# Splitting the rows of maxima on VectorE ahead of the turn, in the first attention stage as in the second

## The reference, cut to what matters

```
x = L0_attn_x                                    # (4, 1024, 128) float32
xn = layernorm(x)
s = L0_attn(xn, ...)                             # 16 heads of 8, bias by relative position
g = silu(L0_ffn(xn, ...))
x = x + s * g
xn = layernorm(x)
s = L1_attn(xn, ...)                             # 8 differential heads, causal
g = silu(L1_ffn(xn, ...))                        # 8 experts, top 2
return x + s * g

def L0_attn(x, Wq, bq, Wk, bk, Wv, bv, Wo, bo, rel_table):
    Q, K, V = proj(Wq, bq), proj(Wk, bk), proj(Wv, bv)
    rel_emb = rel_table[clip(pos[:, None] - pos[None, :] + 127, 0, 254)]
    scores = (einsum('bhid,bhjd->bhij', Q, K) + einsum('bhid,ijd->bhij', Q, rel_emb)) / sqrt(8)
    attn = softmax(scores, axis=-1)
    out = einsum('bhij,bhjd->bhid', attn, V)
    return out @ Wo.T + bo
```

## Time and profile before

| | us |
|---|---|
| median of 3 runs | 2022.06 |
| the 3 runs | 2018.59 to 2034.35 |
| the profiled execution, its own time | 2009.26 |
| its span, first to last instruction | 2007.4 |

### The profile page before, as it was taken

How to read it: one execution, slowest core, us unless ns; L and a number is a source line. 1 busy time by engine, 2 the same in 40 slices (tenths; PEclk the granted TensorE clock), 3 DMA queues, 4 the chain that set the end, 5 groups by cost and what they waited for, 6 DMA issues and landing times. The chain is left out here.

```text
span 2007.4 us, 77167 instructions
## 1 busy us (share of the span) xinstructions
PE 1620.5 (81%) x33422; PEld 1255.6 (63%) x33422; DVE 1322.0 (66%) x1921; ACT 1171.6 (58%) x1500; POOL 1098.2 (55%) x1104
## 2 busy tenths in 40 slices
PE   6888789989999999999997633487778778778776
PEld 4666677777787777788785523376445545555554
DVE  5553767778777767768786342255877677677673
ACT  2333477777787777778785321154556556556555
POOL 4755488888899788978986265001222222222211
PEclk9888799999999999999998665698799799788788
DMA  3355023222332233322221172362121121111100
GB/s 96 97 172 141 24 90 92 75 82 77 103 99 55 82 94 97 86 65 66 74 70 56 57 215 82 100 176 75 40 51 29 44 50 28 49 47 27 30 13 10
DMA packets 189005, 151.47 MB, mean 75 GB/s; under 512 B 92163, under 2 KB 178190, under 8 KB 183166
## 3 DMA queue, kind: packets, MB, share of 16 engines
q1 hardware_dynamic: 161526, 103.80, 18.2%
q10 hardware_dynamic: 20088, 27.00, 4.3%
q0 software_dynamic: 7056, 15.74, 2.7%
HBM read 98.91 MB, written 46.79 MB: 73 GB/s over the span
## 5 line engine op out<-in xcount | busy, mean ns | idle before, releaser
L1876 ACT ACTIVATE a_EX<-bank 128x1024 f32<-128x1024 f32 x624 | 615.0, 1027 | 296.9 <-PE bank L1672 233.0
L2015 DVE TENSOR_TENSOR a_PM<-bank,a_PM 128x1024 f32<-128x1024 f32 x336 | 400.6, 1222 | 121.7 <-PE bank L1672 110.1
L1797 POOL TENSOR_TENSOR a_SN<-a_SN,a_MB 128x1024 f32<-128x1024 f32 x176 | 420.8, 2431 | 41.8 <-DMA a_MB<-m_dram 40.6
L2039 DVE TENSOR_REDUCE a_M<-bank 128x2 f32<-128x1024 f32 (+3 forms) x296 | 330.9, 1163 | 111.2 <-PE bank L1685 74.3
L1975 PE MATMUL bank<-a_EX,VV 128*32 128x128 f32 x9984 | 378.8, 294 | 11.1 <-issue 9.2
L1672 PE MATMUL bank<-QS,KS 51*128 51x128 bf16 (+1 forms) x4992 | 248.4, 233 | 95.0 <-DVE a_M L2039 33.0
L1975 PEld LDWEIGHTS bank<-a_EX,VV 128*32 128x32 f32 x9984 | 279.3, 117 | 62.7 <-issue 36.1
L1672 PEld LDWEIGHTS bank<-QS,KS 51*128 51x128 bf16 (+1 forms) x4992 | 163.9, 101 | 191.0 <-DVE a_M L2039 54.0
L1872 ACT ACTIVATE a_SN<-bank 128x1024 f32<-128x1024 f32 x176 | 176.8, 1024 | 61.0 <-PE bank L1651 59.3
L1651 PE MATMUL bank<-QP,rel_t 112*128 112x32 bf16 x5632 | 198.1, 177 | 3.7 <-issue 3.4
L1880 ACT ACTIVATE a_SN<-a_SN 128x1024 f32<-128x1024 f32 x176 | 184.3, 1058 | 22.8 <-POOL a_SN L1797 22.7
(11 more groups left out here) (213 smaller groups left out, 2286.5 us busy)
## 6 DMA issues: line engine op xcount, KB each, us to landing
a_MB<-m_dram SPq DMA_DIRECT2D x32, 1024.0 KB, 5.3
QS<-q_dram SPq DMA_DIRECT2D x192, 96.0 KB, 3.0
q_dram<-t_PARTS SPq DMA_DIRECT2D x32, 192.0 KB, 3.0
k_dram<-t_PARTS SPq DMA_DIRECT2D x16, 384.0 KB, 3.7
KS<-k_dram ACTq DMA_DIRECT2D x16, 384.0 KB
xs_dram<-bv SPq DMA_DIRECT2D x26, 192.0 KB, 4.8
t_XS<-xs_dram SPq DMA_DIRECT2D x18, 256.0 KB, 4.1
y_dram<-t_Y ACTq DMA_DIRECT2D x18, 256.0 KB, 2.3
```

What stands on the lines that cost most here:

```text
L1797: pool.tensor_tensor(near_view(sn), near_view(sn), as_near(MB[:, :, :], it.part), ALU.add)\
L1876: act.activation(as_banks(EX[:, it.need % ER[layer]], part), by_head, ACT.Exp, scale=SCALE).then_inc(act_done, 1)
L2015: dve.tensor_tensor(pm, mb.rearrange("p hh (k i) -> p hh k i", k=4), pm, ALU.max).then_inc(max_used, 1)
L2039: dve.tensor_reduce(target[:, :, p0:p0 + g], mb[:, :, 0:g * width].rearrange("p hh (k j) -> p hh k j", k=g), AX.X, ALU.max).then_inc(max_u ...
```

## The change

In the first attention stage `maxt` reduces into `MT`, the tile with room for three parts, and behind the second half DVE does what it does in the second stage: cast to bfloat16, subtract, cast the rest, subtract, each with a drain (`split_rows`). PE turns 48 columns instead of 16. ACT copies the turned rows twice: to `MP` in bfloat16 and to `MR` in float32. The step `msplit` on POOL goes. SP sends two DMAs instead of six. `mstore` becomes two DMAs of 8 rows each instead of one of 16. The planner's costs follow: `mstore` 400 to 800, `mcopy` 277 to 540 in this stage, `rows` 4000 to 1600, 1100 more on DVE for the second half of `maxt`, and no POOL step between `mcopy` and the rows. The due times in `AIM` stay.

```diff
-COST = {..., "mstore": 400, ...
-        ..., "mcopy": 277,
+COST = {..., "mstore": 800, ...
+        ..., "mcopy": (540, 277),
...
-        ..., "rows": (4000, 1600), ...
+        ..., "rows": 1600, ...
...
-                taken.append(ring(Step("maxt", u, None, c), COST["maxt"], "dve", COST["take"],
+                taken.append(ring(Step("maxt", u, None, c), COST["maxt"], "dve", COST["take"] + 1100 * c,
...
-        done["msplit", u] = add("pool", Step("msplit", u), COST["split"], [(copied, told)]) if layer == 0 else copied
-        rows = [(add("sp", Step("msplit", u), COST["rows"][layer], [(done["msplit", u], told)]), COST["rows_in"])]
+        done["msplit", u] = copied
+        rows = [(add("sp", Step("msplit", u), COST["rows"], [(done["msplit", u], told)]), COST["rows_in"])]
...
                         if it.kind == "msplit":
-                            sp.wait_ge(m_split if layer == 0 else m_copied, u + 1)
+                            sp.wait_ge(m_copied, u + 1)
                             for hh in range(2):
                                 row = hh * HALF + ROWS
-                                if layer == 0:
-                                    for k in range(3):
-                                        sp.dma_start(QS[row + k:row + k + 1, u % QR, :, hh, :], MP[hh * PAIRS:(hh + 1) * PAIRS, u % 2, k, :])\
-                                          .then_inc(m_in[u % QR], 16)
-                                else:
-                                    sp.dma_start(QS[row:row + 3, u % QR, :, hh, :], MP[hh * 3 * PAIRS:(hh + 1) * 3 * PAIRS, u % 2, :])\
-                                      .then_inc(m_in[u % QR], 16)
+                                sp.dma_start(QS[row:row + 3, u % QR, :, hh, :], MP[hh * 3 * PAIRS:(hh + 1) * 3 * PAIRS, u % 2, :])\
+                                  .then_inc(m_in[u % QR], 16)
...
-                            sp.dma_start(m_dram[u % 2].rearrange("(k hh i) -> hh k i", hh=2, i=P), MR[:, u % 2, :]).then_inc(m_stored, 16)
+                            for hh in range(2):
+                                sp.dma_start(m_dram[u % 2].rearrange("(k hh i) -> hh k i", hh=2, i=P)[hh],
+                                             MR[hh * 3 * PAIRS:hh * 3 * PAIRS + PAIRS, u % 2, :]).then_inc(m_stored, 16)
...
-                        elif it.kind == "msplit":
-                            mp = MP[:, u % 2, :, :]
-                            pool.wait_ge(m_copied, u + 1)
-                            pool.tensor_copy(mp[:, 0], MR[:, u % 2, :])
-                            pool.drain()
-                            pool.tensor_tensor(MS[:, :], MR[:, u % 2, :], mp[:, 0], ALU.subtract)
-                            pool.drain()
-                            pool.tensor_copy(mp[:, 1], MS[:, :])
-                            pool.drain()
-                            pool.tensor_tensor(mp[:, 2], MS[:, :], mp[:, 1], ALU.subtract).then_inc(m_split, 1)
...
-                                    act.wait_ge(m_split, u - 1)
-                                    act.wait_ge(m_stored, 16 * (u - 1))
-                                act.activation(MR[:, u % 2, :], bank[0:H, MISC, 0:P], ACT.Copy, scale=-1.0).then_inc(misc_used, 1)
+                                    act.wait_ge(m_stored, 32 * (u - 1))
+                                act.activation(MP[:, u % 2, :], bank[0:3 * H, MISC, 0:P], ACT.Copy, scale=-1.0)
+                                act.activation(MR[:, u % 2, :], bank[0:3 * H, MISC, 0:P], ACT.Copy, scale=-1.0).then_inc(misc_used, 1)
...
+                    def split_rows(u):
+
+                        top, rest, last = (MT[:, u % 2, :, k, :] for k in range(3))
+                        dve.tensor_copy(MH[:, :, :], top)
+                        dve.drain()
+                        dve.tensor_tensor(rest, top, MH[:, :, :], ALU.subtract)
+                        dve.drain()
+                        dve.tensor_copy(MH[:, :, :], rest)
+                        dve.drain()
+                        dve.tensor_tensor(last, rest, MH[:, :, :], ALU.subtract)
+                        dve.drain()
+                        dve.sem_inc(m_ready, 1)
...
-                            dve.tensor_reduce(M[:, u % 2, :].rearrange("p (hh k) -> p k hh", hh=2)[:, 4 * part:4 * part + 4, :],
+                            dve.tensor_reduce(MT[:, u % 2, :, 0, :].rearrange("p hh k -> p k hh")[:, 4 * part:4 * part + 4, :],
                                               mb.rearrange("p b (k hh j) -> p (b k) hh j", k=2, hh=2), AX.X, ALU.max).then_inc(max_used, 1)
                             if it.last:
                                 dve.drain()
-                                dve.sem_inc(m_ready, 1)
+                                split_rows(u)
```

More of the change, by code:

```diff
@@ L133, in far_keys @@
     return [(0, width)] if width <= 512 else [(0, 512), (512, width)]
-COST = {"far": 270, "near": 1290, "maxt": 880, "mstore": 400, "mb": 700, "av": 930, "mrow": 110, "oback": 440, "oturn": (110, 220), "oproj": (330, 460),
-        "mask": 260, "evict": 1028, "nexp": 1068, "ocopy": 600, "oturned": (277, 400), "mcopy": 277,
+COST = {"far": 270, "near": 1290, "maxt": 880, "mstore": 800, "mb": 700, "av": 930, "mrow": 110, "oback": 440, "oturn": (110, 220), "oproj": (330, 460),
+        "mask": 260, "evict": 1028, "nexp": 1068, "ocopy": 600, "oturned": (277, 400), "mcopy": (540, 277),
         "take": 1221, "nmax": 1600, "nlast": 1900, "split": 1300, "onorm": (613, 2300), "final": (300, 430), "add": (1000, 900), "fetch": 2800, "landed": 3000, "row": 400, "weigh": 1120, "mix": 820, "tanh": 330, "gate": 1800,
-        "nsub": 2560, "perm": 6480, "orms": 5700, "rows": (4000, 1600), "seen": 310, "told": 80, "rows_in": 2100, "mb_in": 5700, "q_in": 3000, "kv": 750}
+        "nsub": 2560, "perm": 6480, "orms": 5700, "rows": 1600, "seen": 310, "told": 80, "rows_in": 2100, "mb_in": 5700, "q_in": 3000, "kv": 750}
 SHAPE = {"max": "rows", "exp": "rows", "av": "columns"}
@@ L216, in attention_tasks @@
         done["mrow", u] = add("pe", Step("mrow", u), COST["mrow"], [(k, ready) for k in taken] + [(last("first", u - 2), 0)])
-        copied = add("act", Step("mcopy", u), COST["mcopy"], [(done["mrow", u], seen), (last("msplit", u - 2), told),
+        copied = add("act", Step("mcopy", u), COST["mcopy"][layer], [(done["mrow", u], seen), (last("msplit", u - 2), told),
                                                               (last("mstore", u - 2), COST["rows_in"])], aimed="msplit")
-        done["msplit", u] = add("pool", Step("msplit", u), COST["split"], [(copied, told)]) if layer == 0 else copied
-        rows = [(add("sp", Step("msplit", u), COST["rows"][layer], [(done["msplit", u], told)]), COST["rows_in"])]
+        done["msplit", u] = copied
+        rows = [(add("sp", Step("msplit", u), COST["rows"], [(done["msplit", u], told)]), COST["rows_in"])]
         exps = {}
@@ L588, in build @@
         XG1 = [32 * (UNITS // 2) * (i < 2) for i in range(XGR)]
-        KV1, V1, Q1, M1, STORED1 = 192 * (B // 2), 16 * (B // 2), 64 * (UNITS // QR), 96 * (UNITS // QR), 16 * (UNITS // 2)
+        KV1, V1, Q1, M1, STORED1 = 192 * (B // 2), 16 * (B // 2), 64 * (UNITS // QR), 32 * (UNITS // QR), 16 * (UNITS // 2)
         def load_q(layer, eng, u):
@@ L1566, in attention_stage @@
                 rms_tmp = local("rms_tmp", [P, 2, PAIRS])
-            if layer == 0:
[L1568 to L1571, removed]
-            else:
-                MT = local("MT", [P, 2, 2, 3, PAIRS])
-                MH = local("MH", [P, 2, PAIRS], BF16)
-                MP = local("MP", [3 * H, 2, P], BF16)
+            MT = local("MT", [P, 2, 2, 3, PAIRS])
+            MH = local("MH", [P, 2, PAIRS], BF16)
+            MP = local("MP", [3 * H, 2, P], BF16)
+            MR = local("MR", [3 * H, 2, P]) if layer == 0 else None
             RC = local("RC", [P, H])
@@ L1586, in attention_stage @@
                 sem(n + s) if layer == 0 else None for s in ("pm_ready", "nsub_done", "nexp_done", "m_stored", "mb_in"))
-            m_ready, m_psum, m_split = sem(n + "m_ready"), sem(n + "m_psum"), sem(n + "m_split")
+            m_ready, m_psum = sem(n + "m_ready"), sem(n + "m_psum")
             act_psum, act_done, av_done = sem(n + "act_psum"), sem(n + "act_done"), sem(n + "av_done")
@@ L1711, in _ @@
                                 sp.wait_ge(mb_in, 16 * (u - 1))
-                            sp.dma_start(m_dram[u % 2].rearrange("(k hh i) -> hh k i", hh=2, i=P), MR[:, u % 2, :]).then_inc(m_stored, 16)
+                            for hh in range(2):
+                                sp.dma_start(m_dram[u % 2].rearrange("(k hh i) -> hh k i", hh=2, i=P)[hh],
+                                             MR[hh * 3 * PAIRS:hh * 3 * PAIRS + PAIRS, u % 2, :]).then_inc(m_stored, 16)
                         if it.kind == "mb":
-                            sp.wait_ge(m_stored, 16 * (u + 1))
+                            sp.wait_ge(m_stored, 32 * (u + 1))
                             if u:
@@ L1948, in _ @@
```

(15 more changed lines are left out.)

2 lines of the change are left out of this document (removed).

## The result

The changed kernel takes 2074.77 us in the median of 4 runs (2068.59 to 2079.45), the kernel before on the same chip 2020.32: a ratio of 1.026, interval 1.023 to 1.030. It is slower by 2.6%, some 53 us; the forecast was 10 us faster, and the range ended at 2055.

A forecast was written before the change was run, and what follows sets the result against it. PE was taken to bound the first attention stage, with 85.6 us idle to win. Terms -6 - 4 - 3 + 3.5 = -9.5, say -10 us, took the median from 2022 to 2012; the 8-in-10 range was 1985 to 2055.

The forecast's parts named there:

- The waits for their DMAs: PE's waits in the first attention stage for the DMAs of the rows of maxima: 15.4 us, to fall under 6.
- the 5.70 us wait: PE's wait for a row in the last but one unit of the first stage; nearly all of it was to go.
- The chain: Steps from ACT's copy of the turned maxima to the last row's issue on SP: 2.8 us against 7.2 before.
- DVE: Split on DVE in the first stage: 83 us more work, of which 3.5 us was to show on PE.
- 48 us of waits for POOL: DVE's split in the first stage: one wait of 1.5 us a unit for a running POOL instruction, over 32 units.
- The terms -6, -4 and -3: PE's gains in us from earlier rows: last but one unit 6, first unit 4, the eight other waits 3.
- the row's 2.18 us wait: PE's wait for a row in the first unit of the first stage; it was to go, within the 4 us term.
- The plan: Redrawn order of the first stage: taken as 0, with 9 us either side, a tenth of PE's 85.6 idle us.
- Wrong by the plan: Sign in PE's first-stage waits: rows' waits as forecast, but others grown, ACT's slots or `av` waiting for near exponentials.

The follow-up runs named there:

- the pairs without the split: Changed kernel, and it planned with rows 3000 ns later and turn one step later, each without DVE's four split instructions: 1.024 against 1.026, 1.001 against 1.003.
- the best plan here, without the split: Changed kernel planned with rows 3000 ns later and PE's turn one step later, DVE's four split instructions left out: 2015.78 us, ratio 1.001.
- the old order: Changed kernel's instructions with the first attention stage in the order of the kernel before, POOL's split dropped from the list: 2068.06 us, ratio 1.025.
- a plan without them: Changed kernel with only the planner's estimate of the rows' landing in the first stage 3000 ns later: 2026.29 us, ratio 1.003.
- the better plans: Changed kernel planned with rows 3000 ns later: 2026.29 us; with the turn also one step later: 2030.81 us; that without DVE's split: 2015.78 us.

## Why the prediction was wrong

**Right in part: the rows.** The waits for their DMAs fell from 15.4 to 1.5 us, the 5.70 us wait is gone, and two issues stand where six were. The chain was worked out as 2.8 us, with the split and the copies in it, as if PE turned the maxima at once. It does not: from the second reduction to the last row it is 6.0 us on the mean, and a row leaves some 2 us earlier in a middle unit (median 8.7 before, 6.5 after), where 3 to 4 were worked out, and 2.9 in the last unit but one, where it was 6. Only the first, 11.5 us earlier, came as worked out (11).

**Not contradicted, but by another way: DVE.** 3.5 us was taken for it, and the pairs without the split differ by about 3.5 us, which is not told from zero. That the sizes agree is luck: 48 us of waits for POOL were assumed; the trace shows 0.11 us at the first cast a unit, 3.7 us in all. By the rule of the Trainium skill (SBUF — State Buffer, section Who interferes with whom) the cast can block for a whole POOL instruction. The longest here took 1.17 us and ended 0.03 us behind a subtraction of POOL, which agrees with the rule; it was seldom met, in 8 of 32 first casts.

**Wrong: what the rows' waits are worth.** The terms -6, -4 and -3 took those waits as won. "What is late next is the slot that DVE or ACT still reads" stood in the text, without a price. In the first unit the row's 2.18 us wait is gone, and in the 30 us behind 225 us PE ran no more matmuls than before (605 against 611). Even the best plan here, without the split, is no faster than before (1.001, interval 1.000 to 1.003): the 15.4 us left one line of the waits, and those for DVE's slots grew from 29.1 to 42.7 us.

**Wrong, and this decided: "The plan. Costs change and due times stay, so the whole order of the stage is drawn anew. No row prices it; I take nothing", with 9 us to either side.** The same instructions in an order planned for rows 3 us later are 2.3% faster, some 46 us, five times that bound. The bound took PE's idle time for what an order can move. A worse order adds idle time without such a limit, and a lower granted clock came with it here (0.93 against 0.96): 37.1 us of new idle time and 27.5 us of slower matmuls. What grew in its place is the wait for slots that DVE or ACT still reads, from 44.8 to 80.9 us. The section on what would show it wrong did name the sign that came ("Wrong by the plan: the same waits but other ones grown, ACT's slots or `av` waiting for near exponentials"), yet no rival carried it.

**Missing: PE at the turn.** The text costed the split in the chain of the rows and in DVE's sum, not on PE, which stands in order behind it. In the old order this is 24.7 us. The new plan, whose costs include the 1100 ns, puts other steps there: PE waits 2.7 us, and the turn, and with it the row, comes later.

Shown is that the order of the changed kernel makes the loss, and that its waits are for slots. That the exponentials ahead of the far maxima are the part of the order that does it fits the place of the waits (19.8 us right behind them) and the fall of the ACT wait from 33.6 to 13.4 us in a plan without them, but no run changed that alone. Why the better plans still wait longer for DVE's slots than the kernel before, split or not, stays open. No run here beat the kernel before.

## What to carry to other kernels

Where the lists are drawn by a planner, a change of its costs is a change of the whole stage: an earlier input can pull steps ahead that then crowd one reader's slots. Price it as a rival of its own, and try the changed instructions with a later estimate before judging them. An operation put between a producer and an in-order consumer is paid by that consumer, unless its list has something else to do there.

## What the runs showed of the hardware

PE can stand for its own instructions. In the old order 18 gaps of 0.6 to 3.1 us, 36.3 us in all, each ended some 1.4 us behind a packet of the instruction queue, and moving one 1 MB broadcast by 1.9 us on the mean halved them. In the waits they appear only as "issue", at a line that changes from unit to unit; the DMA view of the stretch ahead of the gap shows what they are.
